# A ViT block with quantised attention and routed experts: GpSimd makes the third copy of the second norm's last channels, the first loads come in pieces, and ScalarE rounds the attention weights

## What is computed

```python
y = einsum('nsi,oi->nso', patches, W) + b            # embedding 768 -> 192
h = layernorm(y) * ln_w + ln_b                       # norm 1, affine
# attention on layernorm(h) (norm 2): 12 heads of 16, 196 tokens an image
q, k, v = fake_quant(...)                            # round to whole steps, clip to -4..3
attn = fake_quant(q @ k.T / N, s_attn, 0, 7)         # no softmax: scaled, rounded, clipped
h = h + fake_quant(attn @ v, s_after, -4, 3) @ Wproj.T + bproj
# experts on layernorm(h) (norm 3): a router picks one of 8
routes = argmax(route_prob); hdn = gelu(x @ w1[e] + b1[e])
h = h + (hdn @ w2[e] + b2[e]) * route_prob_max
```

## Time and profile before

| | us |
|---|---|
| median of 3 runs (lowest, highest) | 998.43 (997.61, 999.94) |
| the profiled execution: time, and span from first to last instruction | 998.46, 996.7 |
| TensorE matmul busy | 907.5 (91% of the span) |
| VectorE, ScalarE, GpSimd busy | 743.0, 702.9, 510.8 |
| mean granted TensorE clock, share of full speed | 0.972 |

### The profile page before, as it was taken

How to read it: one execution, slowest core, us unless ns; L and a number is a source line. 1 busy time by engine, 2 the same in 40 slices (tenths; PEclk the granted TensorE clock), 3 DMA queues, 4 the chain that set the end, 5 groups by cost and what they waited for, 6 DMA issues and landing times.

```text
span 996.7 us, 24830 instructions
## 1 busy us (share of the span) xinstructions
PE 907.5 (91%) x8170; PEld 785.2 (79%) x8170; DVE 743.0 (75%) x2855; ACT 702.9 (71%) x1516; POOL 510.8 (51%) x890
## 2 busy tenths in 40 slices
PE   5678999999999999998889899999999999999877
PEld 4566888888888888877677788888888888887766
DVE  4677878788788778777676777878878877878563
ACT  1367877777878777776566777777787877777652
POOL 4434564637465564636527456463746556463332
PEclk9797999999999999999999999999999999999889
DMA  7321121212121121212102112121202111000000
GB/s 228 105 64 34 49 64 41 61 45 74 32 69 49 53 65 41 61 45 68 44 25 73 32 53 65 41 64 42 77 29 69 50 53 49 10 13 13 14 13 28
DMA packets 31395, 52.52 MB, mean 53 GB/s; under 512 B 4653, under 2 KB 17949, under 8 KB 31269
## 3 DMA queue, kind: packets, MB, share of 16 engines
q1 hardware_dynamic: 31268, 50.94, 16.7%
HBM read 41.30 MB, written 9.63 MB: 51 GB/s over the span
## 4 chain that ended last, share of the span: by engine, by line
PE 34%; DVE 6%; ACT 6%; issue 5%; POOL 1%; DVEq 0%; ACTq 0%; POOLq 0%
PE mixed_ps L787 7%; PE near_ps L650 6%; PE mixed_ps L777 6%; PE mixed_ps L641 5%; PE scores_ps L708 2%; ACT relu L897 2%; PE near_ps L723 1%; PE turn_ps L663 1%; ACT hid L932 1%; ACT o_b L921 1%; DVE h L1222 1%; PE turn_ps L664 1%; PE mixed_ps L741 1%; DVE k_b L1182 1%; PE mixed_ps L742 1%
## 5 line engine op out<-in xcount | busy, mean ns | idle before, releaser
L897 ACT ACTIVATE relu<-scores_ps,c_prob 98x784 uint16<-98x784 f32 x384 | 348.8, 909 | 139.2 <-PE scores_ps L708 117.3
L650 PE MATMUL near_ps<-we,x_sb 128*128 128x192 f32 x1176 | 258.4, 341 | 12.5 <-DMA const_sb<-in_const 8.2
L978 POOL TENSOR_TENSOR ve<-mv,const_sb 128x1 f32<-128x1 f32 x294 | 60.3, 205 | 360.9 <-DVE mv L1319 357.1
L650 PEld LDWEIGHTS near_ps<-we,x_sb 128*128 128x128 f32 x1176 | 195.2, 196 | 19.1 <-DMA const_sb<-in_const 8.2
L991 POOL TENSOR_TENSOR expd<-econst,below 128x8 f32<-128x8 f32 x98 | 161.9, 1666 | 49.6 <-DVE below L1249 49.6
L981 POOL TENSOR_TENSOR rs<-ve,const_sb 128x1 f32<-128x1 f32 x294 | 173.9, 591 | 23.0
L1160 DVE TENSOR_SCALAR prob<-relu 98x784 bf16<-98x784 uint16 x384 | 151.1, 394 | 9.4 <-ACT relu L897 1.2
L787 PE MATMUL mixed_ps<-w_sb,hid 128*128 128x192 f32 x784 | 145.8, 330 | 0.0
L787 PEld LDWEIGHTS mixed_ps<-w_sb,hid 128*128 128x128 f32 x784 | 125.5, 191 | 1.4
L1135 DVE TENSOR_SCALAR xn<-h,mv,rs 128x192 f32<-128x192 f32 x196 | 74.1, 378 | 33.9 <-POOL rs L981 33.7
L932 ACT ACTIVATE hid<-mixed_ps,b_sb 128x384 f32<-128x384 f32 (+1 forms) x128 | 73.0, 586 | 36.2 <-PE mixed_ps L777 35.7
(11 more groups left out here) (155 smaller groups left out, 2208.2 us busy)
## 6 DMA issues: line engine op xcount, KB each, us to landing
x_sb<-in_x SPq DMA_DIRECT2D x98, 384.0 KB, 3.0
out<-out_sb SPq DMA_DIRECT2D x98, 96.0 KB, 1.6
we<-in_tok_w SPq DMA_DIRECT2D x1, 576.0 KB, 4.3
w_sb<-in_w SPq DMA_DIRECT2D x1, 384.0 KB
hid<-in_w_qkv SPq DMA_DIRECT2D x1, 288.0 KB, 5.5
hid<-in_w_qkv SPq DMA_DIRECT2D x2, 144.0 KB, 5.7
hid<-in_w SPq DMA_DIRECT2D x1, 256.0 KB
hid<-in_w SPq DMA_DIRECT2D x2, 128.0 KB
```

The source lines that it names most:

```text
L650: pe.matmul(dst, x_sb[:, tile % X_RING, j], we[:, j], start=j == 0, stop=False)
L897: act.activation(relu16[:, u % 2], scores_ps[0:KEYS, 2 * (u % VISIT):2 * (u % VISIT) + 2, 0:2 * SEQ], ACT.Relu, scale=c_prob[0:KEYS, :]).t ...
```

## The change

Three things change. First, the third copy (`f_c` rows 0 to 63) moves from ScalarE to GpSimd: a new function there, issued at the end of the slot of the transpose, waits for the same `f_b`; TensorE waits for it by `pool_fc`. Second, the first loads: constants and bias rows go first; weight and tile 0 of the embedding come as 6 + 6 pieces with a semaphore for each pair, and TensorE waits for them piece by piece; meanwhile it multiplies a zeroed `one_t` six times. The affine rows go into the lot `loaded[1]`. Third, ScalarE rounds `wq_hi` (slot 6), VectorE only subtracts (slot 8, now 64 rows instead of 128 in the second), a memset of `wq_lo_b` goes to the start, and six small operations on scales go to slot 22.

```diff
+            def load_first():
+                for j in range(KC):
+                    sync.dma_start(we[:, j], tok_w[:, j]).then_inc(first_in[j], 16)
+                    sync.dma_start(x_sb[:, 0, j], x[0][:, j]).then_inc(first_in[j], 16)
...
-            load(0, bias_loads[1:])
-            load_tile(0)
-            load(1, embed_loads)
-            load(0, bias_loads[:1])
+            load(0, bias_loads)
+            load_first()
             load_tile(1)
-            load(4, affine_loads)
+            load(1, affine_loads)
...
-            come(pe, 0, 1)
+            pe.wait_ge(set_pool, 2)
+            for n in range(WARMS):
+                pe.matmul(mixed_ps[0][:, :], one_t[:, 0:128], one_t[:, 0:512], start=True, stop=True)
...
+            def split_attention():
+                come(act, 2)
+                act.activation(wq_hi_a[:, :], raw_q_a[:, :], ACT.Copy)
+                act.activation(wq_hi_b[:, :], raw_q_b[:, :], ACT.Copy).then_inc(set_act, 1)
...
-                act.wait_ge(act_hi, number + 1)
-                act.activation(f_c[0:LO, g.parity, cols], f_b[0:LO, g.parity, cols].bitcast(f32),
-                               ACT.Copy).then_inc(act_fc, 1)
...
+            def third_copy(g, tile):
+                cols = g.cols2(tile)
+                pool.wait_ge(act_hi, TURN_NO[2, tile] + 1)
+                if tile == g.first2:
+                    wait(pool, up_made, 8 * (g.offset - 1))
+                pool.tensor_copy(f_c[0:LO, g.parity, cols], f_b[0:LO, g.parity, cols].bitcast(f32)).then_inc(pool_fc, 1)
...
             def set_attention():
                 come(dve, 2)
-                split_r(wq_hi_a[:, :], wq_lo_a[:, :], raw_q_a[:, :])
-                split_r(wq_hi_b[:, :], wq_lo_b[:, :], raw_q_b[:, :])
-                setup(dve.memset(wq_lo_b[LO:128, :].bitcast(f32), 0.0))
+                dve.wait_ge(set_act, 1)
+                setup(dve.tensor_tensor(wq_lo_a[:, :], raw_q_a[:, :], wq_hi_a[:, :].bitcast(f32), ALU.subtract))
+                setup(dve.tensor_tensor(wq_lo_b[0:LO, :], raw_q_b[0:LO, :], wq_hi_b[0:LO, :].bitcast(f32), ALU.subtract))
                 setup(dve.reciprocal(rec[:, :], scal[:, :]))
```

More of the change, by code:

```diff
@@ L419, in vit_tower_kernel @@
         mixed_ps = [pb(f"mixed_ps{n}", [128, 512]) for n in range(2)]
-        loaded = [sem(f"loaded{n}") for n in range(5)]
+        loaded = [sem(f"loaded{n}") for n in range(4)]
+        first_in = [sem(f"first_in{j}") for j in range(KC)]
+        set_act = sem("set_act")
         set_dve = sem("set_dve")
@@ L445, in vit_tower_kernel @@
         act_hi = sem("act_hi")
-        act_fc = sem("act_fc")
+        pool_fc = sem("pool_fc")
         dve_lo = sem("dve_lo")
@@ L549, in vit_tower_kernel @@
         bias_loads += [(raw_24[:, EMBED:2 * EMBED], tok_b.partition_broadcast(24))]
-        embed_loads = [(we[:, :, :], tok_w)]
         affine_loads = [(lnw[:, :], ln_w.partition_broadcast(TT)), (lnb[:, :], ln_b.partition_broadcast(TT))]
@@ L565, in vit_tower_kernel @@
         ]
-        all_loads = [bias_loads, embed_loads, attention_loads, expert_loads, affine_loads]
-        SET_EMBED, SET_ATTENTION, SET_ALL = 10, 25, 49
+        all_loads = [bias_loads, affine_loads, attention_loads, expert_loads]
+        SET_EMBED, SET_ATTENTION, SET_SCALES, SET_ALL = 11, 17, 23, 47
         ROUTER_PRODUCT, PREPARE_PROJECTION, PREPARE_EXPERTS = 8, 4, 9
-        PREPARE_ATTENTION = 8
+        SPLIT_ATTENTION, PREPARE_ATTENTION, PREPARE_SCALES, WARMS = 6, 8, 22, 6
         def come(eng, *which):
@@ L645, in embed @@
                 dst = near_ps[0:TT, 0:EMBED]
+                if tile == 0:
+                    pe.wait_ge(first_in[j], 32)
+                elif j == 0:
+                    number = tile // X_RING + (1 if tile % X_RING else 0)
+                    pe.wait_ge(x_in[tile % X_RING], 16 * number)
                 if j == 0:
-                    pe.wait_ge(x_in[tile % X_RING], 16 * (tile // X_RING + 1))
                     empty(pe, "embed", tile)
@@ L771, in up @@
                     pe.wait_ge(spread_out, g.count(2, part + 1))
-                    pe.wait_ge(act_fc, part_tiles(g, part)[-1] + 1)
+                    pe.wait_ge(pool_fc, part_tiles(g, part)[-1] + 1)
                 cols, left = part_cols(g, part), slice(128 * m, 128 * (m + 1))
@@ L810, in body @@
                     for tile in first_at(TURN2, one, s):
+                        if tile == 0:
+                            come(pe, 0)
                         turn(1, tile)
@@ L936, in body @@
                 for s in range(SLOTS):
+                    if one and is_first(one) and s == SPLIT_ATTENTION:
+                        split_attention()
+                    if two and is_first(two) and s == 0:
+                        act.wait_ge(set_dve, SET_SCALES)
                     if two:
@@ L969, in _ @@
             pool.memset(warm[:, :], 0.0).then_inc(set_pool, 1)
+            pool.memset(one_t[:, :], 0.0).then_inc(set_pool, 1)
             pool.memset(v_pad[:, :, :, :, :], 0.0).then_inc(set_pool, 1)
             pool.memset(onehot3[:, :, :], 0.0).then_inc(set_pool, 1)
-            pool.memset(one_t[:, :], 0.0).then_inc(set_pool, 1)
-            come(pool, 0, 4)
+            come(pool, 0, 1)
             def rstd(tile, mv_sem, mv, ve, rs, ve_sem, rs_sem):
@@ L1015, in body @@
                         affine(tile)
+                    for g, tile in second_at(TURN3, two, three, s):
+                        third_copy(g, tile)
             passes(body)
@@ L1044, in set_embedding @@
                 setup(dve.memset(rows24[:, :, :], 0.0))
+                setup(dve.memset(wq_lo_b[LO:128, :].bitcast(f32), 0.0))
                 come(dve, 0)
@@ L1066, in set_attention, with set_scales @@
                 setup(dve.tensor_copy(inv_rows[LO:128, 2:3], rec[LO:128, 1:2]))
+            def set_scales():
                 setup(dve.tensor_scalar(products[:, 0:1], scal[:, 0:1], scal[:, 1:2], DH ** -0.5 / SEQ,
@@ L1329, in body @@
                         assert done[0] == SET_ATTENTION
+                    if one and is_first(one) and s == PREPARE_SCALES:
+                        set_scales()
+                        assert done[0] == SET_SCALES
                     if two and is_first(two) and s == PREPARE_PROJECTION:
```

## The result

The changed kernel takes 989.64 us (median of 7 runs, 987.75 to 991.32); beside it the kernel before took 997.72 us (7 runs, 994.35 to 999.97). The ratio is 0.9916, 95% interval 0.9896 to 0.9935: faster by 0.8%, 2.3 us behind the forecast of 987.3 and inside its range. The profiled execution took 989.64 us with a span of 987.8 us, 8.9 us less than the span before. The right total hides wrong terms, so here the 8.9 us are split by stretch.

What follows compares the result with a forecast made beforehand. TensorE was taken as the bound, busy 53.86 of 56.01 us in a middle pass. Middle passes -6.0, seven-tile passes and tail -1.7, start -3.5 sum to -11.2 us: 998.46 to 987.3 us, likeliest range 982 to 990, with rivals 980 to 994.

Steps and rivals of the forecast that it cites:

- Middle passes, -0.50 each: Twelve passes of 56.01 us: moving the copy gains 0.35 + 0.15 us in each, -6.0 in all (-4.2 to -7.3).
- the first place: TensorE's 0.96 us wait before the scores, ended by the relu behind the third copy: all 0.35 us gained.
- the second place: TensorE's 0.26 us wait, ended by a `y` in a row containing a third copy: 0.15 us gained.
- The copy's price, 0.35 us (0.19 to 0.46): Time of one third copy on GpSimd, bounded by `ve` below and a line through `ve` and `m` above.
- VectorE disturbed: GpSimd at work could slow VectorE's clips; charged nothing, as the copy starts while VectorE reads PSUM for `f_lo`.
- the rival: Second rival: copy near 0.5 us or more, or each stretches a VectorE clip by 0.35 us; 992 us, chance 0.14.
- Seven-tile passes and tail, -1.7: 438 to 575 us and after 911 us: five places where the chain crosses `f_b`, 0.35 us gained at each.
- The start, -3.5: First passes: `xn` earlier -3.0, clock -1.5, scale operations in slot 22 +1.0; bounds about +1 and -6.
- the queue is emptier: I take 3.0: Attention loads at the start: 3.0 us from last issue to landing, out of 3.0 to 6.3, so landed at 19.1.
- The first rival: The start gives nothing: attention lot lands at 22 us or later, clock dips as before; 991 to 992, chance 0.18.
- The clock term, -1.5: Start: less idle time raises TensorE's granted clock for embedding matmuls; half of 2.8 us counted, bounds 0 and -2.8.
- The two rivals in which GpSimd's copy does harm: Copy disturbs VectorE or its own queue: 992, chance 0.14; copy costs like a power, 1.65 us: 1000, chance 0.05.

Runs made afterwards that it cites:

- the copy's own run: The kernel before with only the third copy moved from ScalarE to GpSimd: 993.41 us, ratio 0.9948 (0.9927 to 0.997).
- the start alone: The changed kernel with the third copy put back on ScalarE, so only the new start differs from the kernel before: 995.69 us, ratio 0.9975 (0.9953 to 0.9997).

## Why the prediction was right, and where it was not

The direction, the range and the mechanism (ScalarE no longer makes the copy in front of a relu that TensorE waits for) held. The total was only 2.3 us off because errors had opposite signs, and that is luck: against terms of -6.0, -1.7 and -3.5 the profiled execution shows -3.2, -5.1 and -0.56.

1. *Middle passes, -0.50 each.* It was 0.27. "At the first place nothing else stands between, so all 0.35 us reaches TensorE": right, 0.34. "So of the second place 0.15 us is left": the failed step. Everything that it rests on happened (`nb` 0.10 us late, `n` 0.16 early), but `n` was taken for what TensorE waits for there. It waits for `y`, and `y` for TensorE's own embedding; `n` only has to be out of the way, and the wait's floor is 0.21 us. The earlier trace rows show both, `n` and, in the last row, `y` as the releaser. The third thing, missed: 0.12 us goes back before `down`, where VectorE's `h` is next in line. The prediction named no successor of the stall at place 1.
2. *The copy's price, 0.35 us (0.19 to 0.46).* Measured mean 0.33. The run without a copy shows that the single copy costs the pass nothing.
3. *VectorE disturbed.* It was charged at nothing, and for the single copy that came out: the clips kept their mean of 394 ns. But the effect exists, and in the run with two copies it is what makes the pass longer (0.07 us on a clip, 0.08 on `xn`). VectorE is busy 44.62 us in a middle pass without the copy, 44.84 with it and 45.31 with two each: some 0.04 us for each of six copies, 0.08 for each second one. The Trainium skill's rule (page "GPSIMD Engine Reference", section 8, "Key points": GpSimd and VectorE share SBUF interfaces) agrees in sign with these sums; its size here was a tenth to a quarter of the 0.35 us that the rival took.
4. *Seven-tile passes and tail, -1.7.* It was -5.1. In the seven-tile stretch TensorE's idle time fell from 17.5 to 17.0 us (16.7 in the copy's own run), near the 0.70 of the two copies counted there; the rest of the 1.96 is clock. The idle part repeats (17.5 us in both profiles with the copy on ScalarE, 16.7 to 17.0 in the twelve others). The clock part does not follow the copy: over the same twelve profiles the stretch lasts 133.16 to 138.80 us at a granted clock of 1.00 to 0.95, so those 1.4 us are scatter. In the tail no idle time was won (15.5 before, 15.9 after): if one wait became shorter, others became longer by as much. The 3.2 us came from the clock, which the term did not contain. The stretches of the tail at half clock (1.2 GHz), before and after:

```profile
917.70:927.80 10.10, 9.76 (x53) 8.36 (x54) 7.68 (x29) 4.82 (x9) 6.62 (x7) 0.50 0.01 3
962.10:972.20 10.10, 7.92 (x30) 6.73 (x30) 5.92 (x22) 1.15 (x3) 6.64 (x8) 0.50 0.00 0
```

```profile
947.40:950.70 3.30, 2.98 (x12) 2.93 (x13) 3.05 (x12) 2.26 (x4) 0.98 (x3) 0.50 0.00 0
957.60:964.40 6.80, 6.07 (x19) 4.32 (x16) 2.73 (x7) 1.21 (x2) 4.49 (x6) 0.50 0.00 0
```

   TensorE was busy 9.18 of the 10.10 us and 7.16 of the 10.20 us ahead of the first two, 2.15 of the 3.40 and 4.00 of the 6.80 us ahead of the last two. With the copy on ScalarE the tail's clock was 0.88 in both profiles (85.56 and 85.75 us), without it there 0.90 to 0.94 in all twelve others (82.4 to 84.3 us, mean 83.1). So the copy's move goes with a gain of some 2.6 us in the tail, and the 3.16 of the changed kernel's profile is one of the larger samples of it. Which wait of the tail decides the clock was not tried and stays open, and with it why the move has this effect.
5. *The start, -3.5.* It was -0.56 in the profile; at the medians the start alone gave 2.7 us (0.3 to 4.7). `xn` did come earlier (24.66 instead of 26.36; 23.4 was forecast), and the roundings took the 1.4 us forecast (0.68 and 0.67). Two steps failed. "Ten more issues" moved not only the attention lot but tile 3 behind it: the prediction called its lateness "a new short wait", and it was 3.03 us, and filled the place of the stall that was removed. And "the queue is emptier: I take 3.0": the last load of the lot was issued earlier than forecast (at about 14.8, not 15.6 to 16.6), but took 5.7 us to land, hardly less than the 6.3 before, so ScalarE waited for the projection weights until 20.61 and not 19.1. The first rival (chance 0.18, 991 to 992) had the lot at 22 or later and a clock as low as before; neither came, but its conclusion that the start gives almost nothing fits this profile. The clock term, -1.5, came in part: 0.83 and 0.83 instead of 0.84 and 0.65 over 20 to 40 us (0.75 to 0.83 over 30 to 40 us in the five profiles of this start). The scales in slot 22 cost 0.80 us (1.0 forecast), shown by the wait for `a_b` at 50.08 that disappears when they go back.

The two rivals in which GpSimd's copy does harm did not come true for one copy. The break-even between the powers, put at 1.3 us, lies above the two copies (0.7 us with the gap between them), which still gained 0.13 us a pass over the kernel before; where it lies was not measured.

## What to carry to other kernels

Ask of each stall that a change removes what TensorE would wait for next, and give that wait a number: here it was a tile issued behind the moved loads, a projection weight in the same semaphore's lot, and a bank that VectorE empties. Every piece into which a load is split costs its issue to everything behind it in the queue, and a consumer should wait for a lot that holds nothing but what it reads. Work moved to GpSimd has to be priced on VectorE too: where VectorE runs without a gap on the way to what TensorE needs, its stretched rows come out of the time one for one. Before a gain is credited to the instructions that moved, compare TensorE's granted clock and idle time by stretch, since one may have changed without the other.

## What the runs showed of the hardware

- Most issues on SyncE's queue take 0.43 us, and 0.47 from start to start, whether they move 64 KB or 384 KB (others in the first 24 us of the changed kernel 0.28 to 0.64): twelve pieces in the changed kernel hold the queue from 2.59 to 8.16 us. The Trainium skill (page "DMA: Bandwidth & Descriptors", section "Issuing engines are not separate DMA queues") calls the time to initiate a DMA "usually small relative to the DMA itself"; this trace agrees only in part. For pieces of 64 and 96 KB the issue is a fifth of the time from issue to landing (0.43 of 1.9 and 2.1 us), and the loads behind all twelve are issued 3.5 us later than before.
- GpSimd's copy of 64 x 128 elements takes 0.28 us at best and 0.33 on average, about what ScalarE took for it (0.31 in the earlier trace rows). A second copy right behind it stretched VectorE's clip beside it from 0.36 to 0.43 us and `xn` from 0.37 to 0.45, and itself took 0.41.
- In the tail TensorE's busy time changed without its idle time: 15.5 and 15.9 us idle with 70.1 and 66.6 us busy for the same 550 matmuls. The runs of one kernel here differ by up to 1% (993.46 to 1003.18 us for the kernel before in one sitting), and their mean granted clock goes the same way: 0.971 to 0.974 in those above 999 us, 0.979 to 0.981 in the four below 995.
